# Second attention of a fused two-layer kernel: the exponential of one step in eighteen moves to VectorE, and the whole steps of a block come before the diagonal ones

## The reference

```python
q, k, v = (proj(Wq, bq), proj(Wk, bk), proj(Wv, bv))      # b, H=16, t=1024, HD=8
attn = jnp.einsum('bhqd,bhkd->bhqk', q, k) * scale
attn = attn + alibi
attn = jnp.where(causal, attn, jnp.finfo(x.dtype).min)
p = jax.nn.softmax(attn, axis=-1)
out = jnp.einsum('bhqk,bhkd->bhqd', p, v).transpose(0, 2, 1, 3).reshape(b, t, c)
return out @ Wo + bo
...
x = x + s * g
```

## Time and profile before

| | |
|---|---|
| median of three runs | 921.98 us (921.61, 921.98, 923.97) |
| span of the profiled execution, first to last instruction | 919.9 us |
| TensorE, busy share of the span | 87% |
| ScalarE | 90% |
| VectorE | 44% |
| GpSimd | 23% |
| mean granted TensorE clock | 0.973 |

### The profile page before, as it was taken

The page is one execution under the profiler, slowest core; times in us unless marked ns, Lnnn a source line. Parts: engine busy times, 40 slices in busy tenths (PEclk is TensorE's granted clock), DMA queues, the critical chain, the costliest instruction groups (busy, mean ns, idle before and its releaser), DMA issues. The chain is left out here.

```text
span 919.9 us, 23162 instructions
## 1 busy us (share of the span) xinstructions
PE 797.0 (87%) x9838; PEld 321.5 (35%) x9838; DVE 406.8 (44%) x878; ACT 830.0 (90%) x919; POOL 208.2 (23%) x261
## 2 busy tenths in 40 slices
PE   3759999899999999998999988755888888978977
PEld 2312434334343443433334433212333333333333
DVE  7731264444747446474545777880120121121122
ACT  7659999999999999999999956556999999899996
POOL 2201110130202212121311202002234334324333
PEclk9979999999999999999999999986999999999999
DMA  6872020200200302103000034010112022022000
GB/s 180 285 265 44 2 74 2 69 7 2 97 25 12 110 2 74 48 1 120 2 1 25 24 92 165 0 46 1 36 40 86 19 68 86 1 86 86 1 13 25
DMA packets 32049, 53.52 MB, mean 58 GB/s; under 512 B 5576, under 2 KB 16456, under 8 KB 31944
## 3 DMA queue, kind: packets, MB, share of 16 engines
q1 hardware_dynamic: 31944, 52.02, 18.1%
HBM read 31.29 MB, written 20.71 MB: 57 GB/s over the span
## 5 line engine op out<-in xcount | busy, mean ns | idle before, releaser
L983 ACT ACTIVATE a_probs<-a_sc 128x1024 f32<-128x1024 f32 x512 | 474.3, 1032 | 9.6 <-PE a_sc L1182 9.0
L1855 ACT ACTIVATE a_probs<-a_sc 128x1024 f32<-128x1024 f32 x288 | 269.7, 1044 | 23.9 <-PE a_sc L2007 17.6
L1197 PE MATMUL a_o<-a_probs,vt 128*18 128x256 f32 (+1 forms) x3072 | 271.8, 457 | 0.0
L2042 PE MATMUL a_o<-a_probs,vt 128*18 128x256 f32 (+3 forms) x1856 | 154.6, 442 | 0.9
L1182 PE MATMUL a_sc<-q_st,k_st 32*128 32x512 f32 x1024 | 131.1, 500 | 23.4 <-ACT a_probs L983 17.7
L2001 PE MATMUL a_sc<-q_st,k_st 32*128 32x512 f32 (+3 forms) x768 | 79.3, 428 | 56.8 <-ACT a_probs L1855 45.2
L1881 POOL TENSOR_SCALAR_AFFINE_SELECT a_probs<-a_probs 128x512 f32<-128x512 f32 x128 | 80.3, 645 | 194.8 <-ACT a_probs L1855 194.8
L1197 PEld LDWEIGHTS a_o<-a_probs,vt 128*18 128x18 f32 x3072 | 65.5, 97 | 142.9 <-issue 102.7
L1182 PEld LDWEIGHTS a_sc<-q_st,k_st 32*128 32x128 f32 x1024 | 50.6, 184 | 137.6 <-ACT a_probs L983 128.6
L1010 POOL TENSOR_TENSOR early<-early 128x512 f32<-128x512 f32 x32 | 38.4, 1199 | 182.3 <-DVE early L1120 182.3
L2001 PEld LDWEIGHTS a_sc<-q_st,k_st 32*128 32x128 f32 x768 | 37.3, 187 | 117.0 <-ACT a_probs L1855 98.1
(11 more groups left out here) (242 smaller groups left out, 757.2 us busy)
## 6 DMA issues: line engine op xcount, KB each, us to landing
q_st<-q_hl SPq DMA_DIRECT2D x48, 256.0 KB
k_st<-k_hl SPq DMA_DIRECT2D x48, 256.0 KB
q_hl<-parts SPq DMA_DIRECT2D x12, 512.0 KB, 4.4
k_hl<-parts SPq DMA_DIRECT2D x12, 512.0 KB, 4.9
q_hl<-early SPq DMA_DIRECT2D x4, 512.0 KB, 4.8
k_hl<-early SPq DMA_DIRECT2D x4, 512.0 KB, 5.6
out_dram<-x SPq DMA_DIRECT2D x7, 256.0 KB, 3.8
x<-in_L_attn_x_dram SPq DMA_DIRECT2D x3, 512.0 KB, 5.9
```

The costliest lines, as they stand in the source:

```text
L983: nc.scalar.activation(probs[t % RING][:, 2 * pair:2 * pair + 2, :], scores[unit % SLOTS][:, :, :], ACT.Exp).then_inc(expd, 1)
L1197: ins = nc.tensor.matmul(o_ps[32 * h:32 * h + 2 * W9, c0:c1], vt[b % 2][:, kt, gp, h, W9 * gs:W9 * gs + 2 * W9], probs[t % RING][:, h, c0: ...
L1855: nc.scalar.activation(probs[t % RING][:, 2 * pair:2 * pair + 2, :], scores[unit % SLOTS][:, :, :], ACT.Exp).then_inc(expd, 1)
L2042: ins = nc.tensor.matmul(o_ps[32 * h:32 * h + 2 * W9, q0:q0 + w], vt[b % 2][:, kt, gp, h, W9 * gs:W9 * gs + 2 * W9], probs[t % RING][:, h, ...
```

## The change

In each group two units, u12 (first half of s6) and u15 (second half of s7), are computed by VectorE instead of ScalarE. It scales and shifts the scores out of PSUM into 32-bit integers (`take`, which releases the slot by the semaphore `taken`), then works in SBUF: six `power_op`s of 128 x 1024 for each unit (two bit operations, then four scalar_tensor_tensor of two SBUF tensors each) that make the exponential of them. They are spread over pairs 3 to 8 of the group by `POWER_AT`. ScalarE's other halves of s6 and s7 go into one buffer of the ring, whose product takes two different key blocks (`swapped`), and the product of the two units of VectorE is added by `held_product`, one step of four matmuls, in the first pair of the next group. Besides, the blocks of s5 to s17 now stand as eight whole steps, then five diagonal ones.

```diff
--- before.py
+++ after.py
...
@@ -1718,6 +1719,17 @@
 CORNER = 96
 STEEP = 1
 
+HELD = 6
+HELD_OUT = 9
+GROUP_STEPS = 18
+HELD_UNITS = (2 * HELD, 2 * HELD + 3)
...
+POWER_OPS = 6
+
 
 def causal_steps():
 
@@ -1734,7 +1746,7 @@
                         ([(gs, own + 1, P, 0, 3 * P), (gs, own + 3, 3 * P, 3 * P, P)], (0, 3))]
 
             shared = [([(gs, own + 2, 2 * P, 2 * P * gs, 2 * P) for gs in range(2)], (0, 2))]
-            blocks = whole(0) + diagonal(0) + shared + diagonal(1) + whole(1)
+            blocks = whole(0) + whole(1) + diagonal(0) + shared + diagonal(1)
             for n, (pieces, masked) in enumerate(blocks):
                 steps.append((gp, qh, pieces, masked, n == 0, n == len(blocks) - 1))
     return steps
@@ -1767,6 +1779,7 @@
     LAST = S // 2 + 2
     TANH_AT = (16, 18)
     GATE_AT = (10, 11)
+    POWER_AT = ((3, 4, 4, 5, 5, 5), (6, 6, 6, 7, 7, 8))
 
     def fill_index(kind, b, hf):
         return next(n for n, one in enumerate(fills) if one[0:3] == (kind, b, hf))
...
@@ -1814,6 +1830,15 @@
         def tail_tiles(k):
             first = BT * (B - 1) + HT + 2 * k
             return slice(first, first + 2)
+
+        def by_vector(unit):
+            return unit % (2 * GROUP_STEPS) in HELD_UNITS
+
+        def taken_count(unit):
+            return sum(by_vector(u) for u in range(unit + 1))
+
+        def exp_count(unit):
+            return unit + 1 - taken_count(unit)
 
         with nc.Block() as block:
             @block.sync
@@ -1851,8 +1876,14 @@
                         act.wait_ge(pv_done, t - RING + 1)
                     for pair in range(2):
                         unit = 2 * t + pair
+                        if by_vector(unit):
+                            continue
+                        home = t
+                        if r % GROUP_STEPS == HELD:
+                            home = t + 1
+                            act.wait_ge(pv_done, home - RING + 1)
                         act.wait_ge(scored, unit + 1)
-                        nc.scalar.activation(probs[t % RING][:, 2 * pair:2 * pair + 2, :],
+                        nc.scalar.activation(probs[home % RING][:, 2 * pair:2 * pair + 2, :],
                                              scores[unit % SLOTS][:, :, :], ACT.Exp).then_inc(expd, 1)
                     for hf in range(2):
                         if r == TANH_AT[hf]:
@@ -1875,7 +1906,7 @@
                     columns = plan[t % PER1][3]
                     if not columns:
                         return
-                    pool.wait_ge(expd, 2 * t + 2)
+                    pool.wait_ge(expd, exp_count(2 * t + 1))
                     for n in columns:
                         part = probs[t % RING][:, :, n * P:(n + 1) * P]
                         ins = pool.affine_select(out=part, in_=part, compare_op=ALU.is_ge, fill=0.0, base=0,
@@ -1955,6 +1986,34 @@
                     banks = scores[k][:, :, 0:C]
                     nc.vector.tensor_tensor(mix[1][:, 2 * k:2 * k + 2, :], banks, s["y"][:, tail_tiles(k), :], ALU.mult).then_inc(gained, 1)
 
+                power = Chain(dve, powered)
+
+                def take(g, j):
+
+                    unit = 2 * GROUP_STEPS * g + HELD_UNITS[j]
+                    dve.wait_ge(scored, unit + 1)
+                    nc.vector.tensor_scalar(bits[:, 2 * j:2 * j + 2, :].bitcast(U32), scores[unit % SLOTS][:, :, :],
+                                            BITS_PER_E, BITS_OF_ONE, ALU.mult, ALU.add).then_inc(taken, 1)
+
+                def power_op(g, j, k):
+
+                    y, out = bits[:, 2 * j:2 * j + 2, :], held[:, 2 * j:2 * j + 2, :]
+                    m = fraction[:, :].rearrange("p (n t) -> p n t", n=2)
+                    if k == 0:
+                        dve.wait_ge(taken, 2 * g + j + 1)
+                        if g > 0 and j == 0:
+                            dve.wait_ge(pv_done, GROUP_STEPS * g)
+                        ins = nc.vector.tensor_scalar(m.bitcast(U32), y.bitcast(U32), FRACTION, ONE, ALU.bitwise_and, ALU.bitwise_or)
+                    elif k == 1:
+                        ins = nc.vector.tensor_scalar(y.bitcast(U32), y.bitcast(U32), EXPONENT, None, ALU.bitwise_and)
+                    elif k < POWER_OPS - 1:
+                        power.wait()
+                        ins = nc.vector.scalar_tensor_tensor(out, m if k == 2 else out, QUARTIC[k - 2], m, ALU.add, ALU.mult)
+                    else:
+                        power.wait()
+                        ins = nc.vector.scalar_tensor_tensor(out, out, QUARTIC[k - 2], y, ALU.add, ALU.mult)
+                    power.mark(ins)
+
                 nc.vector.memset(o_ps[:, :], 0.0).then_inc(o_clear, 1)
                 e = 0
                 for pair in range(LAST):
@@ -1971,6 +2030,13 @@
                     for hf in range(2):
                         if b < B and r == GATE_AT[hf]:
                             gate(b, hf)
+                    group, at = divmod(pair, GROUP_STEPS // 2)
+                    for j in range(2):
+                        if group < 2 * B and at == HELD // 2:
+                            take(group, j)
+                        for k in range(POWER_OPS):
+                            if group < 2 * B and at == POWER_AT[j][k]:
+                                power_op(group, j, k)
                 dve.wait_ge(pv_done, S)
                 settle_last(0)
                 settle_last(1)
@@ -1991,9 +2057,11 @@
                     banks = [scores[(2 * t + i // 2) % SLOTS][:, i % 2, :] for i in range(G)]
                     if opens and qh == 0:
                         pe.wait_ge(staged[gp], 16 * LOADS * (b + 1))
-                    for unit in (2 * t, 2 * t + 1):
-                        if unit >= SLOTS:
-                            pe.wait_ge(expd, unit - SLOTS + 1)
+                    for unit in (2 * t - SLOTS, 2 * t + 1 - SLOTS):
+                        if unit >= 0 and by_vector(unit):
+                            pe.wait_ge(taken, taken_count(unit))
+                        elif unit >= 0:
+                            pe.wait_ge(expd, exp_count(unit))
                     for n, (gs, kt, q0, at, w) in enumerate(pieces):
                         for i in range(G):
                             part = slice(STACK * i, STACK * i + STACK)
@@ -2026,24 +2094,35 @@
                     gp, qh, _, columns, opens, closes = plan[r]
                     pieces = shares(t)[share]
                     first, last = share == 0 or not shares(t)[0], share == 1 or not shares(t)[1]
-                    if not pieces:
+                    if not pieces or r % GROUP_STEPS == HELD:
                         return
                     if first:
                         if columns:
                             pe.wait_ge(masked, masked_count(t))
                         else:
-                            pe.wait_ge(expd, 2 * t + 2)
+                            pe.wait_ge(expd, exp_count(2 * t + 1))
                         if opens and t > 0:
                             pe.wait_ge(o_free, ENDS * b + closing.index(next(c for c in closing if c >= r)))
                         if b > 1 and r == 0:
                             pe.wait_ge(v_rdy, b - 1)
+                    swapped = r % GROUP_STEPS == HELD + 1
                     for n, (gs, kt, q0, at, w) in enumerate(pieces):
                         for h in range(G):
+                            k = kt - 1 if swapped and h >= 2 else kt
                             ins = nc.tensor.matmul(o_ps[32 * h:32 * h + 2 * W9, q0:q0 + w],
-                                                   vt[b % 2][:, kt, gp, h, W9 * gs:W9 * gs + 2 * W9], probs[t % RING][:, h, at:at + w],
+                                                   vt[b % 2][:, k, gp, h, W9 * gs:W9 * gs + 2 * W9], probs[t % RING][:, h, at:at + w],
                                                    start=opens, stop=closes and last and n == len(pieces) - 1, tile_position=(0, 32 * h))
                     if last:
-                        ins.then_inc(pv_done, 1)
+                        ins.then_inc(pv_done, 2 if (r + 1) % GROUP_STEPS == HELD else 1)
+
+                def held_product(g):
+
+                    b, gp = divmod(g, 2)
+                    gs, kt, _, _, _ = plan[GROUP_STEPS * gp + HELD][2][0]
+                    pe.wait_ge(powered, 2 * POWER_OPS * (g + 1))
+                    for h in range(G):
+                        nc.tensor.matmul(o_ps[32 * h:32 * h + 2 * W9, :], vt[b % 2][:, kt if h < 2 else kt + 1, gp, h, W9 * gs:W9 * gs + 2 * W9],
+                                         held[:, h, :], start=False, stop=False, tile_position=(0, 32 * h))
 
                 def piece_of(n, kind, b, hf, piece, pieces):
                     if piece == 0:
@@ -2069,6 +2148,8 @@
                         piece_of(*one)
                     if 2 * pair < S:
                         score(2 * pair + 1)
+                    if 2 * pair >= GROUP_STEPS and 2 * pair % GROUP_STEPS == 2 * HELD_OUT % GROUP_STEPS:
```

(4 more changed lines are left out.)

6 lines of the change are left out of this document (added).

## The result

| | before | after |
|---|---|---|
| median of 4 runs each, us | 922.48 (921.61 to 923.97) | 967.17 (963.81 to 968.38) |
| profiled span, us | 919.9 | 966.6 |
| mean granted TensorE clock | 0.973 | 0.942 |

The change makes the kernel 4.75% slower (ratio 1.0475, interval 1.0454 to 1.0496): 45 us, where 31 were forecast. 967 lies 1 us above the range (931 to 966).

What follows compares the result with a forecast made beforehand. A step was held bound equally by ScalarE's throughput and the even-unit slot loop, 1.82 us each. Terms 1.8 + 5.1 + 20.6 - 0.9 + 4.4 = +31 on the median 922.0 gave 953 us, range 931 to 966.

Steps and rivals of the forecast that it cites:

- the held product: At entry to the next group, four 512-wide matmuls and a wider product s17 delay the scores of s2: +5.1 us.
- The removal gives nothing: At s6 to s9, taking 16 exponentials off ScalarE gains 0, and the scores of s7 start 0.14 us later.
- the loop of even units: Even unit, release of its slot, next scores: 1.82 us a step, as long as ScalarE's two exponentials.
- the rival by ScalarE's throughput: At s6 to s8, 16 exponentials at 0.91 us give back 14.6, so 907 us; chance of faster 0.07.
- the first part's +1.8: Removed exponentials and the late transpose and product behind them, s6 to s9: 5 x 0.14 + 3 x 0.38 us.
- Masks, update, port: At group ends, masks queue behind the update and alternate with VectorE's long operations, delaying the next scores: +20.6 us.
- The row 787.65: Starting time for the gp 0 half's clock in batch 2, from which s12 was put at 793.1 us.
- the port as the likeliest failure: If VectorE finishes before s14's masks, or turns are taken otherwise, the 20.6 us at group ends shrinks towards 3.6.
- masks pass freely: Rival at the group ends: the port costs little, total +10.6, 932.6 us; chance 0.21.
- The tail: After the last group, late masks make the last products finish at 916.9 instead of 912.47 us: +4.4.
- Idle time up by 45: Sign in the profile after: ScalarE's idle time before exponentials rises by 45 us; under 20 would mean wrong.
- Busy time down by 15: Sign in the profile after: 272 exponentials on ScalarE, busy 15 us less.

Runs made afterwards that it cites:

- e5: The changed kernel plus three spare 512-wide matmuls in each group where TensorE waits for the masks of s15; 954.42 us, ratio 1.0335.
- e7: The kernel before with the exponential of u15 of each group left out and nothing in its place; 922.96 us, ratio 1.0003.
- e6: The kernel before with the exponential of u12 of each group left out and nothing in its place; 919.47 us, ratio 0.9958.
- e4: The changed kernel with GpSimd's update of x moved from behind the mask of s14 to behind that of s17; 934.45 us, ratio 1.0104.
- e3: The changed kernel without VectorE's six operations behind each pass, so part of the exponential is left out; 935.79 us, ratio 1.0134.
- e2: The changed kernel with the old order of blocks, masks at s9 to s13 and the update behind them; 931.02 us, ratio 1.0075.

## Why the prediction was right, and where it was wrong

The measured 967 lies outside 931 to 966. The step that failed is the timing of what follows the stall, in the term *the held product* (+5.1): the sum laid the held product and products s16 and s17 at the durations of 2.4 GHz directly behind 3 us of idle TensorE, and put the clock at nothing without a reason. What the runs showed in its place: TensorE at 0.50, for 6.8 us at five group ends, 10.2 at one and 3.4 at the tail, and 12.8 us gone when spare matmuls keep the clock up (e5). The late start of the stage, 3.8 us in the profiled runs, had no term either; its cause stays open.

- **The removal gives nothing.** Right. e7 (0) and e6 (-3.4) show that the loop of even units sets the step there, and that an exponential outside of it is worth nothing; the rival by ScalarE's throughput (907) is dead. From u11 to u16 it takes 4.52 to 4.58 us in after and 4.53 to 4.60 before. In after the scores of s7 start 1.91 behind those of s6, against 1.81 before, +0.10 for the +0.14 forecast, and of the first part's +1.8 little is to be seen.
- **Masks, update, port: +20.6.** Right in mechanism, and some 13% below the forecast in size: at the place u0 is 3.23 and 3.38 late for 3.4 and 3.2, but part of that is the clock. In e5, at full clock, u0 comes 3.12 late into three gp 0 halves and 2.66 into three gp 1 halves. Before, u0 of a gp 1 half started 0.13 ahead of the end of the record before it, which counts as late too, and after's first group adds 0.2: together 17.9 for the 20.6. The row 787.65 that the prediction counts from stands in no view, but drops out, because both ends of its 3.2 are counted from it. The Trainium skill (SBUF — State Buffer, "SBUF: two separate sides") has one hold the other up for the whole instruction; by that rule, with nothing overlapped, the term would have been 27. The rows keep to the exclusion, and stand on the side of the overlapped handovers: the update ends at 786.60, 0.14 before 785.46 + 1.28. The prediction named the port as the likeliest failure. It was not, and "masks pass freely" (932.6) fell with masks of 1.18 to 1.23.
- **The held product: +5.1.** Here the sum failed. It took 0.87, 0.66 and 0.44 for the products, durations of rows at 2.4 GHz, and laid them directly behind 3 us in which TensorE had nothing to do. At full clock they are right: u4 waits 1.33 in e5 and in e4, where in the kernel before the same exponential waits 0.27, so +1.06 for the forecast 0.99; and the one entry of after into a gp 1 half without a fall of the clock costs 0.56 for 0.52, the others 1.9 to 2.2. At 1.2 GHz the waits of 0.33 and 1.33 become 0.81 and 3.14. The prediction's own numbers had TensorE idle for 3 us a group.
- **The tail: +4.4.** Measured 5.7 (last exponential to the end 15.6, 9.9 before), with the clock at 1.2 GHz for 3.4 us in it. Whether all of the 1.3 is the clock was not tried.
- **The sum.** In profiled spans 46.7 = 3.8 before the stage (it starts at 630.42, not 626.59) + 37.2 in it + 5.7 behind it. The medians lie 44.7 apart, 2 less: the profiled run of before is among its shortest and that of after (968.37) among its longest. e5's span of 954.7 is 34.8 above before's; without the 3.5 by which its stage starts late that is 31.3, the forecast's 31. This match is in part luck, since it holds the 2.2 and 2.9 that e5 adds and terms that came out smaller than forecast. So the two missing terms are the clock and the late start, which the prediction knew nothing of.
- **What was forecast of the trace.** Idle time up by 45: it is up by 48.9, but by only 38.8 in e5 (to 62.7), so that the clock made up for terms that came out smaller, and the number is near by luck. Busy time down by 15: by 11.8, since an exponential behind idle time adds its whole 1.03 to the busy time, and one that follows another only 0.91. VectorE's long operations were to take 1.8 beside the masks; they take 1.53. ScalarE's idle time before u14 and u16 was to be 0.5 or more; it is 0.3 and 0.74.

The terms were added as though each stood by itself. They do not: e3 and e4 each remove one cause, and each takes away more than 30 of the 45.

## What to carry to other kernels

- Before work is taken off the busiest engine, follow one period of the loop in which slots are released. If it is as long as the engine's own period, work left out outside of it is worth nothing (u15: 0), and work left out of it less than its time (u12: 3.4 of 7.3 us). A wait split between the halves of its users gave 3.6 us, and no kernel with VectorE's exponential came below the one before.
- Of a step that is moved, ask what now stands behind it in its queue. Mask, update, mask was the expensive order; mask, mask, update (e4) leaves the kernel with a quarter of the loss.
- A forecast that leaves TensorE idle for some 3 us has to price what follows at 1.2 GHz too, from rows taken at that clock. Where the wait can't be removed, spare matmuls in it can pay (12.8 us here, although they cost 2.2 at the one end of a group that had no such wait).

## What the runs showed that I had not expected

- A stall of TensorE of some 3 us goes with 6.8 us or more at 0.50, six group ends of six in after; with e4's waits of 0.6 to 1.3 us the clock falls once behind the first group, for 3.4 us near 800 us, and before it falls once too (792.0), without such a stall. The Trainium skill (TensorE: Matmul & The Clock Gate, "Why this matters for your kernels") says that idle gaps of TensorE between bursts of matmuls bring back its lower clock; the trace agrees.
- VectorE's integer operations on 1024 elements from SBUF take 0.67 to 0.69 us, half of the 1.23 of the pass from PSUM or of the first long operation.
- The time of one kernel moves by some 3 us between runs, with the granted clock: e2 took 929.13 and 929.17 at 0.971, 932.86 and 932.97 at 0.966. In after's profile TensorE is at half clock for 20.5 us from 52.8, where before it is for 13.7 from 54.7, and for 6.8 us from 544.3, where before it is for 3.4 from 542.8; both lie ahead of every changed instruction. Why the profiled runs of the kernels with VectorE's exponential all start the stage late stays open. By my estimate some 2 to 4 of the 45 us hang on it: 3.8 in the profiled runs, 2 less if the medians are taken.
